# A graph network layer: TensorE's wait for the high half moves from behind the bias matmul to in front of it

## The reference

```python
h = x
for W, b, g, beta in layers:                  # 8 layers, W is 512 x 512
    agg = segment_sum((h * norm_out)[src], dst) * norm_in
    out = agg @ W + b
    h = gelu(layer_norm(out, g, beta))
return layernorm(x + h)
```

## Time and profile before

| | |
|---|---|
| Time, median of 3 runs | 1611.01 us (1607.53 to 1611.39) |
| The profiled execution, its own time | 1612.99 us |
| Its span, first to last instruction | 1610.70 us |
| Granted TensorE clock, mean | 0.834 of 2.4 GHz |
| TensorE matmuls | 1140.8 us busy, 71% of the span |
| VectorE | 915.6 us, 57% |
| GpSimd | 870.6 us, 54% |
| ScalarE | 491.4 us, 31% |
| L1252, the bias matmul, 168 times | 84.6 us, mean 504 ns |
| L1256, 672 times | 288.3 us, mean 429 ns |
| L1257, 672 times | 270.5 us, mean 403 ns |
| L1261, 672 times | 184.5 us, mean 397 ns |

### The profile page before, as it was taken

The page is one execution under the profiler, slowest core; times in us unless marked ns, Lnnn a source line. Parts: engine busy times, 40 slices in busy tenths (PEclk is TensorE's granted clock), DMA queues, the critical chain, the costliest instruction groups (busy, mean ns, idle before and its releaser), DMA issues.

```text
span 1610.7 us, 30805 instructions
## 1 busy us (share of the span) xinstructions
PE 1140.8 (71%) x6235; PEld 865.5 (54%) x6235; DVE 915.6 (57%) x2206; ACT 491.4 (31%) x833; POOL 870.6 (54%) x1092
## 2 busy tenths in 40 slices
PE   7865386796796777976977896789778899950000
PEld 7643133765666656656656665766577676730000
DVE  6644676454463454544654564346543366658997
ACT  5332220433333223323323333333234333320110
POOL 1754201555456356455556465646567566658885
PEclk9655568898897898888989998999999999985555
DMA  0940001614416226135136225522266512249997
GB/s 12 363 166 2 2 1 41 182 59 151 130 72 197 71 97 203 53 130 158 59 126 190 77 78 180 172 77 76 99 199 189 150 72 78 78 152 357 392 395 290
DMA packets 98950, 224.52 MB, mean 139 GB/s; under 512 B 15408, under 2 KB 15408, under 8 KB 98880
## 3 DMA queue, kind: packets, MB, share of 16 engines
q0 software_dynamic: 34432, 104.72, 21.4%
q1 hardware_dynamic: 64448, 119.06, 20.2%
HBM read 137.91 MB, written 85.82 MB: 139 GB/s over the span
## 4 chain that ended last, share of the span: by engine, by line
PE 54%; POOL 13%; issue 10%; DMA 10%; DVE 6%; ACT 3%; ACTq 2%; DVEq 1%; POOLq 1%; SPq 0%
PE ps_y L1256 12%; PE ps_y L1257 10%; PE ps_y L1261 10%; PE ps_a L1236 8%; DMA rows<-h_rows,slot 7%; POOL agg_t L518 5%; POOL rows L460 5%; PE ps_y L1252 4%; POOL agg_t L525 3%; PE ps_a L1151 2%; DVE agg_t L640 2%; ACT agg_t L1005 2%; PE ps_a L1217 1%; DMA w_raw<-in_bs 1%; PE ps_y L1170 1%
## 5 line engine op out<-in xcount | busy, mean ns | idle before, releaser
L1236 PE MATMUL ps_a<-sel,rows 128*128 128x128 f32 x2560 | 368.4, 301 | 182.7 <-DMA rows<-h_rows,slot 120.3
L1236 PEld LDWEIGHTS ps_a<-sel,rows 128*128 128x128 f32 x2560 | 337.6, 211 | 215.1 <-issue 212.3
L468 POOL TENSOR_TENSOR s_lo<-agg_t,s_hi 128x512 fp32r<-128x512 f32 x168 | 217.3, 1295 | 297.0 <-ACT s_hi L1047 297.0
L460 POOL DMA_INDIRECT rows<-h_rows,slot x290 | 278.8, 961 | 152.1 <-issue 111.7
L1042 ACT ACTIVATE agg_t<-ps_a 128x508 f32 x320 | 190.7, 596 | 388.3 <-PE ps_a L1236 367.6
L1256 PE MATMUL ps_y<-w_hi,s_hi 128*128 128x512 f32 x672 | 288.3, 429 | 10.1 <-ACT s_hi L1047 10.1
L815 DVE TENSOR_SCALAR sel<-iota,by_tile 128x128 f32<-128x128 f32 x344 | 123.8, 364 | 285.9 <-PE ps_a L1236 208.5
L1257 PE MATMUL ps_y<-w_lo,s_hi 128*128 128x512 f32 x672 | 270.5, 403 | 0.0
L888 DVE BATCH_NORM_STATS2 small<-ps_y 128x6 f32<-128x512 f32 x168 | 117.4, 699 | 172.1 <-PE ps_y L1261 171.0
L1261 PE MATMUL ps_y<-w_hi,s_lo 128*128 128x512 f32 x672 | 184.5, 397 | 0.0
L1256 PEld LDWEIGHTS ps_y<-w_hi,s_hi 128*128 128x128 f32 x672 | 129.6, 193 | 75.3 <-issue 52.5
(11 more groups left out here) (204 smaller groups left out, 1311.8 us busy)
## 6 DMA issues: line engine op xcount, KB each, us to landing
h_rows<-rows SPq DMA_DIRECT2D x168, 256.0 KB, 2.0
h_rows<-agg_t SPq DMA_DIRECT2D x1, 20480.0 KB, 59.2
agg_t<-in_x SPq DMA_DIRECT2D x78, 256.0 KB, 5.8
out<-agg_t SPq DMA_DIRECT2D x78, 256.0 KB, 5.4
w_raw<-in_Ws SPq DMA_DIRECT2D x32, 256.0 KB, 3.0
rows<-h_rows,slot POOLq DMA_INDIRECT x290, 3.7
rows<-in_ln_g SPq DMA_DIRECT2D x8, 256.0 KB, 3.7
rows<-in_ln_b SPq DMA_DIRECT2D x8, 256.0 KB, 4.5
```

The lines of the kernel that those rows point to most:

```text
L460: g.indirect_dma_start(out=rows[:, k, :], out_offset=None, in_=table[:, :], in_offset=bass.IndirectOffsetOnAxis(ap=slot[:, k:k + 1], axis=0))\
L468: g.tensor_tensor(s_lo[:, k, :, :], agg_t[:, :, bass.ds(c * P, P)], s_hi[:, k, :, :].bitcast(f32), ALU.subtract).then_inc(lo_ok, 1)
L1236: m = mm(ps_a[k % GS][:, b, :], rows[:, k, b * P:(b + 1) * P], sel[:, k % GS, :], start=True, stop=True)
```

## The change

The wait for the high half, with its increment, goes in front of the bias matmul. Nothing else differs.

```diff
                         j = base + c
                         pe.wait_ge(t_ok, done(j + k - 1))
                         pe.sem_inc(pe_tick, 1)
-                        mm(ps_y[k][:, :], ones2[:, :], b_rows[:, :], start=True, stop=False)
                         pe.wait_ge(hi_ok, done(j + k + 1))
                         pe.sem_inc(pe_tick, 1)
+                        mm(ps_y[k][:, :], ones2[:, :], b_rows[:, :], start=True, stop=False)
                         for b in range(KB):
                             mm(ps_y[k][:, :], s_hi[:, k, b, :], w_hi[:, b, :], start=False, stop=False)
                             mm(ps_y[k][:, :], s_hi[:, k, b, :], w_lo[:, b, :], start=False, stop=False)
```

## The result

| | before | after |
|---|---|---|
| Median | 1609.61 us (19 runs, 1606.26 to 1615.88) | 1614.54 us (19 runs, 1611.27 to 1618.83) |
| Ratio | | 1.0031, 95% interval 1.0022 to 1.0040 |
| The profiled execution, its own time | 1612.99 us | 1611.27 us |
| Its span | 1610.70 us | 1609.40 us |
| Granted clock, mean | 0.834 | 0.837 |

The change costs 5.0 us (1609.61 x 0.0031; 3.5 to 6.4 us by the interval). The profiled execution of before lies in the upper half of that kernel's runs and the one of after is the shortest of its own, so their spans say nothing on the cost; what they are good for is single tiles.

What follows compares the result with a forecast made beforehand. TensorE's product stage was taken to bound the kernel. Nothing from 160 tiles plus 3.1 us of exposed bias in 8 first tiles (6 x 0.38 + 2 x 0.43) took 1611.01 to 1614.1 us, range 1610.5 to 1618.0.

Steps and rivals of the forecast that it cites:

- 160 tiles, nothing to gain or lose: Product-stage tiles after each layer's first: the moved wait is already met, so it costs and gains nothing.
- the lead of 2.6 us: Mid-stage tiles: ScalarE's high half is written 2.6 us before the bias matmul starts, so holding the bias is free.
- the low half's wait without a gap: Between L1257 and L1261: an identical met wait, where the next matmul still starts 0.23 us after the last.
- The gap goes with the bias matmul's shape: Mid-stage: 0.31 us a tile lost around the 2-row bias matmul comes from its shape, so moving the wait gains nothing.
- rival D: 160 tiles: the wait itself broke the matmul stream, so moving it gains 49.6 us, giving 1564.5 us; chance 0.05.
- Exposed bias in 8 first tiles, 3.1 us: Each layer's first tile: the bias matmul leaves the wait's shadow and delays what follows, 6 x 0.38 + 2 x 0.43 us.
- the 0.38 of the sum: First tiles at the low clock, six of eight layers: 0.71 us of bias delay is 0.38 us once made good.
- If the clock rises at the same moment as before: First tiles: with an unchanged clock rise, low-clock work is made good at the high clock, 0.71 us becoming 0.38.
- Rival B: Stage starts: later starts lengthen low-clock stretches, 1.6 us per layer; two such layers give 1617.3 us; chance 0.22.
- the sign that was named for B: Profile after the change: a low-clock stretch two rows long at the start of layers 2, 6 or 8.
- Rival C: Layers 3, 4, 5 and 7: later starts meet the same clock rise, returning up to 2.8 us; 1611.3 us; chance 0.17.
- The wait's row: TensorE's wait list: the 10.1 us high-half wait moves before the bias, growing to about 16 us or partly becoming issue.

Runs made afterwards that it cites:

- mid_late: Kernel before with the new order (bias behind the wait) in all tiles but each layer's first, first pair of tiles ahead of the loop: 1609.45 us, ratio 0.9986.
- bias128: Kernel before, wait in the old place, with the bias matmul padded by zeros from 2 to 128 rows: 1545.62 us, ratio 0.9595.
- warm_early: Kernel before with 9 filling matmuls in TensorE's pause ahead of each product stage: 1599.56 us, ratio 0.9929.
- warm_late: Changed kernel with 9 filling matmuls in TensorE's pause ahead of each product stage: 1603.18 us, ratio 0.9954 to the kernel before.
- head_late: Kernel before with the new order in each layer's first tile alone, first pair of tiles ahead of the loop: 1615.92 us, ratio 1.0030.
- head_bias5: `head_late` with five bias matmuls instead of one in each layer's first tile: 1628.84 us, ratio 1.0122 to the kernel before.
- head_twice: `head_late` with one more 2-row bias matmul ahead of the wait, where the old one had been: 1616.77 us, ratio 1.0049 to the kernel before.
- bias128_warm9: `bias128` with 9 filling matmuls in TensorE's pause ahead of each product stage: 1527.49 us, ratio 0.9494 to the kernel before.
- bias128_warm_late: `bias128_warm9` with the wait moved in front of the bias matmul: 1536.48 us, ratio 0.9533 to the kernel before.

## Why the prediction was right

The forecast was 1614.1 us and the measured median 1614.54; but with 19 runs the median of before is 1609.61, not 1611.01, so what should be compared is +3.1 against +5.0 us. That is 0.31%, on the border that was drawn between no change and slower, where the chances stood at 0.72 and 0.23. That the two times agree to 0.4 us is luck: a starting value 1.4 us too high made up for most of a cost put 1.9 us too low, and 3.1 lies below the measured interval of 3.5 to 6.4 us.

- *160 tiles, nothing to gain or lose.* Shown: the mid-stage rows are the same, and `mid_late` is not slower. Neither the lead of 2.6 us nor the low half's wait without a gap was misread.
- *The gap goes with the bias matmul's shape.* Shown by `bias128`; rival D is refuted by the changed kernel's own mid-stage tiles, which keep 3.38 us with 0.43 and 0.34, and by `bias128`, where the gaps close with the wait left in place. The size was off: 0.31 us a tile were counted between bias and second high matmul, 0.43 were there, the front of the bias among them.
- *Exposed bias in 8 first tiles, 3.1 us.* Right: 3.3 us by the stage starts of `warm_early` and `warm_late`; and `head_late` carries the whole cost. At the low clock the bias cost 0.41 to 0.43 us a stage where the low clock lasted as long, and not the 0.38 of the sum.
- *"If the clock rises at the same moment as before".* This is the step of the sum that did not hold. `head_bias5` shows that it rises later with more exposed bias work. In the traces with an early bias and no fillers (before, `mid_late`) the stage starts hold 39.9 and 38.6 us of low clock; in those with an exposed one (after, `head_late`, `head_twice`) 38.1, 47.3 and 45.4. The means differ by 4.3 us, times 0.47 that is 2.0 us, the size of what is missing between 3.1 and 5.0. The profile of after, with 38.1, has no more of it than before has. The granted clocks on record reach further than single traces: their mean is 0.8309 over the 19 executions of after and 0.8300 over the 12 of `head_late`, against 0.8331 over the 12 of `mid_late` and 0.8331 over 43 executions of the kernel before. The direction is thus borne out; but these are means over the whole span, so they give no price, and the remaining 1.7 us or so are a fitting account and not shown.
- *Rival B.* Half right. More long low stretches do go with an exposed bias: 10 of the 16 starts of before and `mid_late` have one, and 21 of the 24 of after, `head_late` and `head_twice`. But the sign that was named for B was worthless. It came, in layers 2 and 6 of the profile after, while layers 1, 7 and 8 went the other way, and it stands in layers 2 and 8 of `mid_late` too, whose bias is not exposed. Reading from one execution which layer would turn was of no use.
- *Rival C* gave back up to 2.8 us from later starts; with +5.0 measured and an interval from 3.5, that is refuted.
- *The wait's row.* About 16 us were expected in front of the bias, "or put partly down to issue"; it is 31.2, since the pause that had been booked as issue is now booked on the same wait.

## What to carry to other kernels

Ask of a moved wait in which tiles it is felt, and price those alone: here 8 of 168, and a free wait in the other 160. A gap in a stream of matmuls next to a wait need not come from the wait: look whether an identical wait elsewhere leaves one, and whether the shape changes there. A bias matmul with 2 rows cost 0.43 us a tile more than the same one padded with zeros to 128 rows; padding it, and filling TensorE's pause ahead of the product with 9 idle matmuls, took this kernel from 1609.16 to 1527.49 us.

## What the runs showed of the hardware

- In a stream of 128-row matmuls of 512 columns at the high clock, 0.227 us apart, a 2-row matmul makes a tile of 13 last 3.37 instead of 2.95 us, with gaps on both sides of it, and the weight load on either side is not taken ahead. The 65 us that padding gave are 4% of the kernel. Several 2-row matmuls in a row (`head_bias5`) leave no gap among themselves.
- One matmul in a pause can go with a clock that stays up or make no difference: with a 128-row one in the pause, which is 2.1 us long without it, the clock was 1.00 in all 8 stages, and without it 4 of 8 fell low (`bias128_warm9` against `bias128_warm_late`, one trace each; 6.3 us by the ratios). A 2-row one in the longer pause without the fillers did nothing (`head_twice`), and with the fillers three low stretches were left (`warm_early`). Whether the number of rows, the length of the pause or the denser stream makes the difference stays open; no run here changes one of them alone.
- Waits that are already met are free in TensorE's stream: in `bias128` there are three of them a tile, and the matmuls start 0.227 us apart throughout.
